# Turning the first half's results with transposing DMA transfers in a fused convolution and feed-forward kernel

## The chip, the cores and the metric

The kernel runs on one core of a Trainium2 chip. The metric is the time of one execution on the device in microseconds (us), as the median of a few runs; lower is better. One further execution was recorded by the profiler.

## What is computed

The input x is 32 sequences of 64 channels by 1024 positions. A state-space layer first convolves each channel along the sequence with a kernel that is generated from a few parameters, masked by each sequence's length. Its result, seen as 2048 tokens of 1024 values, goes through a gated feed-forward layer with 4-bit weights in groups of 128:

```python
gate = x2 @ Wg          # 1024 -> 2752
up = x2 @ Wu
inter = gate * jax.nn.sigmoid(gate) * up
out = (inter @ Wd).astype(jnp.float16)
x = x + out             # the residual: the layer's input, float32
```

`Wg`, `Wu` and `Wd` are unpacked as `q * s[group] - (z[group] + 1) * s[group]`. Only the last cast, to float16, and the residual sum matter for this change.

## The kernel before

**Stages.** Up to about 180 us the kernel generates the convolution kernels and convolves. From there to about 1160 us it runs the feed-forward layer, on two halves of 1024 tokens one after the other (`hf` 0 and 1). Each half has `NT` = 22 tiles of 128 intermediate columns (the last, `TAIL`, has 64), so there are `TILES` = 44 tiles `tau`. A tile has eight steps `g`. In each step TensorE issues four matmuls of `gate(tau, g)`, four of `down` for a unit that lies `LAG` = 11 steps back, and four of `up(tau, g)`. A number n = 8 tau + g - 11 counts the steps of `down`.

**Down units.** A unit is one block of 128 output columns (`hid`) for all 1024 tokens of the half. TensorE writes it into one of two PSUM buffers, `down_ps[0]` and `down_ps[1]`, in turn. VectorE takes it (`take_down`: multiply by the scale, add to `acc`) and signals `down_taken`. TensorE may begin a unit when the unit two before it is taken. `acc` has the output columns on the partitions and the tokens along the row.

**The first half's results.** After tile 21's units, GpSimd casts `acc` to float16 in `o16` (`cast_out`, 8 blocks), while VectorE starts the second half's sums in `acc`. `o16` still has output columns on the partitions; the output wants tokens there. So `turn_out(j)`, j = 0 to 3, has TensorE transpose two blocks of 128 tokens, 8 transposes of 128x128 each, into a `down_ps` buffer. Such a turn is put between a `down` unit and the `up` matmuls, at n = `TURN_AT` + 8 j (181, 189, 197, 205), which is step g = 0 of tiles 24 to 27. It counts as a unit of `down_ps`, hence `down_at` and `turn_at`. VectorE's `finish(j)` adds the two turned blocks to x, which lies in the four slots of `x_fin`, and SP stores them and loads the next two blocks of x.

**VectorE in a tile.** In each step it takes one down unit. After it, by step: g = 0 is preceded by `multiply` (sil times up); g = 1, 3, 5 unpack the next gate, up and down weights (`shift`); g = 2, 4, 6 subtract their zero points (`center`) and write the weights.

**SP's queue.** One queue issues every load and store of this stage, in the program's order. For each tile it loads gate weights for tile tau + 1, up weights, and down weights of tile tau: a transfer of 512 KB (`q_in`) and one of 256 KB (`z_in`) each, into a ring of `QRING` = 4 slots. A load waits until the load four before it has been centered (`centered`). After tile tau's loads, in tiles 25 to 28, come the stores of two finished blocks and loads of two further blocks of x (those of x up to block 7).

Of the kernel before, what the change touches and what calls it, by code (L numbers as in the profile page):

```python
# [9 lines left out]
F16 = mybir.dt.float16  # L10
# [3 lines left out]
ALU = mybir.AluOpType  # L14
ACT = mybir.ActivationFunctionType

P = 128
# [16 lines left out]
NT = 22  # L34
# [3 lines left out]
NH = HID // P  # L38
ROWS = G * NT
LAG = 11  # L40
QRING = 4
TURN_AT, TURN_STEP = 181, 8
SPLIT_FROM = 4
TINY = float(2.0 ** -60)

# [60 lines left out]
    return tau - tau // NT  # L106


def turns_before(n):

    return sum(TURN_AT + TURN_STEP * j < n for j in range(4))


def down_at(tau, hid):

    n = NH * tau + hid
    return n + turns_before(n)


def turn_at(j):  # L120
    return TURN_AT + TURN_STEP * j + 1 + j


def up_after(tau):
# [34 lines left out]
def build_program(nc, x, itok, log_dt, C, log_A, A_imag, D, gq, gs, gz, uq, us, uz, dq, ds, dz,  # L159
# [5 lines left out]
    with ExitStack() as ctx:  # L165
        def sb(name, shape, dt=F32):
            return ctx.enter_context(nc.sbuf_tensor(name, shape, dt))

        def sem(name):
            return ctx.enter_context(nc.semaphore(name))  # L170
# [75 lines left out]
        z_in += [sb(f"z_in{i}", [P, G, P], BF16) for i in range(2, QRING)]  # L246
        w["d"][1] = sb("wd1", [P, HID], F32R)
        staged = sb("staged", [P, HALF], F32R)

        ai_loaded, c_loaded, d_loaded = sem("ai_loaded"), sem("c_loaded"), sem("d_loaded")  # L250
        tab_in, ident_in_sb, lens_in = sem("tab_in"), sem("ident_in_sb"), sem("lens_in")
# [27 lines left out]
        down_mm, down_taken = sem("down_mm"), sem("down_taken")  # L279
        high_staged, high_stored, low_ready = sem("high_staged"), sem("high_stored"), sem("low_ready")  # L280
        high_in = [sem(f"high_in{i}") for i in range(KT)]
        o16_done = sem("o16_done")
        x_fin_in = [sem(f"x_fin_in{i}") for i in range(8)]
        last_mid, last_high, last_low = sem("last_mid"), sem("last_high"), sem("last_low")
        last_mm, last_taken = sem("last_mm"), sem("last_taken")
# [52 lines left out]
        def _(sp):  # L338
# [126 lines left out]
            def load_x(hf, tt):  # L465
                sp.dma_start(x_slot(hf, tt), x_rows(hf * HALF_G + tt)).then_inc(x_fin_in[tt if hf else tt % 4], 16)

            def store_out(hf, tt):
                dst = bass.AP(out.tensor, (hf * HALF_G + tt) * (HG * L), [[H * L, B], [L, HG], [1, L]])
                sp.dma_start(dst, x_slot(hf, tt)).then_inc(out_stored[tt % 4], 16)  # L470

            sp.wait_ge(x1_split, HALF_G)
            sp.wait_ge(scales_ready, 1)
            load_weights("d", 0)
# [2 lines left out]
            for tau in range(1, TILES):  # L477
                if tau + 1 < TILES:
                    load_weights("g", tau + 1)
                if up_after(tau) is not None:  # L480
                    load_weights("u", up_after(tau))
                if tau == NT:
                    sp.wait_ge(high_stored, 16 * KT)
                    for kt in range(KT):
                        sp.wait_ge(gate_mm, 2 * (G * TAIL + kt) + 2)
                        sp.dma_start(high[:, kt, :].bitcast(F32), high_back[kt]).then_inc(high_in[kt], 16)
                load_weights("d", tau)
                if SPLIT_FROM <= tau < SPLIT_FROM + KT:
                    sp.wait_ge(high_staged, tau - SPLIT_FROM + 1)
                    sp.dma_start(high_back[tau - SPLIT_FROM], staged[:].bitcast(F32)).then_inc(high_stored, 16)  # L490
                if tau == NT:
                    for tt in range(4):
                        load_x(0, tt)
                if NT + 3 <= tau < NT + 7:
                    for tt in range(2 * (tau - NT - 3), 2 * (tau - NT - 3) + 2):
                        if tt % 2 == 0:
                            sp.wait_ge(out_ready, tt // 2 + 1)
                        else:
                            sp.wait_ge(down_taken, turn_at(tt // 2) + 1)
                        store_out(0, tt)  # L500
                        if 2 <= tt < 6:
                            sp.wait_ge(out_stored[tt - 2], 16)
                            load_x(0, tt + 2)

            for tt in range(4):
                sp.wait_ge(out_stored[tt], 16 * 2)
# [220 lines left out]
        def _(dve):  # L727
# [281 lines left out]
                to = x_slot(1, tt)  # L1009
                dve.tensor_tensor(to, last_turn_ps(tt), to, ALU.add).then_inc(last_added, 1)  # L1010

            def finish(j):

                at = turn_at(j)
                dve.wait_ge(down_mm, at + 1)
                for i in range(2):
                    tt = 2 * j + i
                    dve.wait_ge(x_fin_in[tt % 4], 16 * (tt // 4 + 1))
                    to = x_slot(0, tt)
                    dve.tensor_tensor(to, down_ps[at % 2][:, i, :].bitcast(F16), to, ALU.add  # L1020
                                      ).then_inc(out_ready if i == 0 else down_taken, 1)

            dve.wait_ge(tab_in, 16)
            arguments(0)
# [33 lines left out]
            for tau in range(TILES):  # L1058
                for g in range(G):
                    if g == 0 and tau and tau != NT:  # L1060
                        multiply(tau - 1)
                    if g == G - 1 and tau == TAIL:
                        multiply(tau)
                    if g == G - 1 and tau == LAST:
                        multiply_last(0)
                        multiply_last(1)
                    n = G * tau + g - LAG
                    if n >= 0:
                        take_down(n // NH, n % NH)
                    if g == 5 and tau == TAIL:  # L1070
                        shift("d", TAIL)
                    if g == 0 and tau == NT:
                        center("d", TAIL)
                    if TURN_AT <= n < TURN_AT + 4 * TURN_STEP and (n - TURN_AT) % TURN_STEP == 0:
                        finish((n - TURN_AT) // TURN_STEP)
                    if tau == 0:
                        if g < G - 1:
                            scale_first_up(g)
                        if g < 6:
                            m, at = (("d", 0), ("g", 1), ("u", 1))[g // 2]  # L1080
                            if g % 2 == 0:
                                shift(m, at)
                            else:
                                center(m, at)
                        continue
                    if tau + 1 < TILES:
                        if g == 1:
                            shift("g", tau + 1)
                        if g == 2:
                            center("g", tau + 1)  # L1090
                    if up_after(tau) is not None:
                        if g == 3:
                            shift("u", up_after(tau))
                        if g == 4:
                            center("u", up_after(tau))
                    if tau == TILES - 1:
                        if g == 1:
                            shift("d", tau)
                        if g == 2:
                            center("d", tau)  # L1100
                    elif not is_tail(tau):
                        if g == 5:
                            shift("d", tau)
                        if g == 6:
                            center("d", tau)
# [9 lines left out]
        def _(pe):  # L1115
# [172 lines left out]
            def rows_second(tt):  # L1288

                taken_before(NH)  # L1290
                for hid in range(NH):
                    mm = pe.matmul(sum_ps(tt)[:, hid // 4, P * (hid % 4):P * (hid % 4) + P],
                                   o16[:, hid, P * tt:P * tt + P], ident16[:], start=False, stop=True,
                                   skip_group_check=True)
                mm.then_inc(sum_mm, 1)
# [5 lines left out]
                    mm = pe.transpose(last_turn_ps(tt)[:, P * hid:P * hid + P], o16[:, hid, P * tt:P * tt + P], ident16[:])  # L1301
                mm.then_inc(last_turned, 1)

            def turn_out(j):

                at = turn_at(j)
                if j == 0:
                    pe.wait_ge(o16_done, NH)
                    pe.wait_ge(ident16_ready, 1)
                pe.wait_ge(down_taken, at - 1)  # L1310
                for i in range(2):
                    to = down_ps[at % 2][:, i, :].bitcast(F16)
                    for hid in range(NH):
                        mm = pe.transpose(to[:, P * hid:P * hid + P],  # L1314
                                          o16[:, hid, P * (2 * j + i):P * (2 * j + i) + P], ident16[:])
                mm.then_inc(down_mm, 1)

            pe.wait_ge(k_sb_ready, NCH)
            for tau in range(TILES):
                for g in range(G):  # L1320
                    n = G * tau + g - LAG
                    if tau == NT and g == 0:
                        down(n // NH, n % NH)
                        gate(tau, g)
                    else:
                        gate(tau, g)
                        if n >= 0:
                            down(n // NH, n % NH)
                    if TURN_AT <= n < TURN_AT + 4 * TURN_STEP and (n - TURN_AT) % TURN_STEP == 0:
                        turn_out((n - TURN_AT) // TURN_STEP)  # L1330
                    if not is_tail(tau):
                        up(tau, g)
            for hid in range(NH - 3, NH):
# [50 lines left out]
```

## Time and profile before

| | |
|---|---|
| Median of 3 runs | 1186.89 us (1185.52 to 1187.82) |
| The profiled execution's own time | 1186.11 us |
| Its span in the trace | 1184.3 us |
| TensorE busy | 1155.2 us (98%) |
| VectorE busy | 891.4 us (75%) |
| ScalarE busy | 848.6 us (72%) |
| DMA queue of SP | 172.95 MB, 50.8% of 16 engines |

A matmul's duration overlaps with the next one's, so the time that TensorE spends on a piece of work is read from the starts of the instructions around it, not from the durations. "SPq" is SP's issuing of a transfer; the time "to landing" runs from the issue to the end of the transfer. The time of a transfer's issue is taken on SP, in which nothing else is issued.

### The profile page before, as it was taken

The numbers are of one execution on the slowest core, as the hardware profiler recorded it, in microseconds if no ns is written. First come the engines' busy times: TensorE is split into PE (matmuls) and PEld (weight loads), VectorE is DVE, ScalarE is ACT, GpSimd is POOL, SyncE is SP. The second block draws the span as 40 slices with busy tenths as digits, with TensorE's granted clock in tenths as the row PEclk, the third lists the DMA queues.
The fourth block names the chain that finished last, engine by engine and source line by source line (L and its number), as shares of the span: only waits on it lengthen the run. The fifth ranks groups of instructions, "written<-read, shape, count | busy, mean of one in ns | idle before, by whom it ended". The sixth has DMA issues, their size and how long they took to land.

```text
span 1184.3 us, 15015 instructions
## 1 busy us (share of the span) xinstructions
PE 1155.2 (98%) x5562; PEld 952.6 (80%) x5562; DVE 891.4 (75%) x964; ACT 848.6 (72%) x1396; POOL 221.0 (19%) x136
## 2 busy tenths in 40 slices
PE   5899999999999999999999999999999999999996
PEld 4899998788788878878878878888888888888883
DVE  6698854777777777777777898887777777777775
ACT  6533212888788788788878797778788788788773
POOL 0022000211332332121121241211211211211213
PEclk9899999999999999999999999999999999999999
DMA  8587868531464366434443775555434434444514
GB/s 296 159 267 247 286 200 266 145 81 54 116 162 114 108 163 158 130 100 107 107 107 95 239 206 153 163 177 143 107 103 111 107 103 111 107 101 113 151 48 166
DMA packets 66975, 173.94 MB, mean 147 GB/s; under 512 B 11654, under 2 KB 17222, under 8 KB 66902
## 3 DMA queue, kind: packets, MB, share of 16 engines
q1 hardware_dynamic: 66870, 172.95, 50.8%
q8 instruction: 44, 0.72, 0.2%
q14 instruction: 29, 0.24, 0.1%
q0 software_dynamic: 32, 0.03, 0.0%
HBM read 159.94 MB, written 15.83 MB: 148 GB/s over the span
## 4 chain that ended last, share of the span: by engine, by line
PE 92%; SPq 3%; DVE 2%; DMA 1%; issue 1%; POOL 0%; ACT 0%; DVEq 0%; POOLq 0%
PE pair L1211 27%; PE pair L1232 26%; PE pair L1252 26%; PE pair L1166 10%; DMA toep<-kernel_padded 1%; SPq L352 1%; DMA kernel_padded<-k_sb 0%; PE pair L1146 0%; POOL o L591 0%; DVE arg L746 0%; DVE y_nat L881 0%; PE pair L1281 0%; PE pair L1314 0%; SPq L377 0%; DVE turns L841 0%
## 5 line engine op out<-in xcount | busy, mean ns | idle before, releaser
L985 DVE SCALAR_TENSOR_TENSOR acc<-pair,s_down,acc 128x1024 f32<-128x1024 f32 x328 | 420.5, 1283 | 197.8 <-PE pair L1252 197.4
L667 ACT ACTIVATE pair<-pair,ratio 128x512 f32<-128x512 f32 x616 | 381.7, 665 | 100.5 <-PE pair L1211 100.2
L686 ACT ACTIVATE pair<-pair,ratio 128x512 f32<-128x512 f32 x581 | 360.2, 659 | 122.0 <-PE pair L1232 121.9
L1211 PE MATMUL pair<-high,wg 128*128 128x512 f32 x704 | 278.8, 396 | 0.0
L1211 PE MATMUL pair<-low,wg 128*128 128x512 f32 x704 | 276.5, 393 | 0.0
L1232 PE MATMUL pair<-high,wu 128*128 128x512 f32 x672 | 267.7, 398 | 0.4 <-DVE sil L963 0.4
L1252 PE MATMUL pair<-mid_h,wd 128*128 128x512 f32 x688 | 267.7, 391 | 0.0
L1252 PE MATMUL pair<-mid_l,wd 128*128 128x512 f32 x672 | 264.7, 394 | 0.0
L1232 PE MATMUL pair<-low,wu 128*128 128x512 f32 x672 | 263.2, 392 | 0.0
L543 POOL CAST mid_h<-sil 128x1024 fp32r<-128x1024 f32 (+1 forms) x43 | 45.1, 1049 | 695.7 <-DVE sil L963 685.0
L1211 PEld LDWEIGHTS pair<-high,wg 128*128 128x128 f32 x704 | 132.1, 188 | 31.7 <-ACT pair L667 1.1
L1232 PEld LDWEIGHTS pair<-high,wu 128*128 128x128 f32 x672 | 126.1, 188 | 38.5 <-issue 10.6
L1211 PEld LDWEIGHTS pair<-low,wg 128*128 128x128 f32 x704 | 132.8, 189 | 29.3
L1166 PE MATMUL pair<-u_all,toep 128*128 128x256 f32 (+7 forms) x1024 | 151.7, 310 | 4.5 <-DMA toep<-kernel_padded 4.5
L1166 PEld LDWEIGHTS pair<-u_all,toep 128*128 128x128 f32 x1024 | 147.0, 193 | 8.8 <-DMA toep<-kernel_padded 4.9
L1252 PEld LDWEIGHTS pair<-mid_h,wd 128*128 128x128 f32 x688 | 129.1, 188 | 30.1
L1252 PEld LDWEIGHTS pair<-mid_l,wd 128*128 128x128 f32 x672 | 126.2, 188 | 29.3
L1232 PEld LDWEIGHTS pair<-low,wu 128*128 128x128 f32 x672 | 126.3, 188 | 27.1
L923 DVE TENSOR_SCALAR q_in<-q_in,shifts 128x1024 int32<-128x1024 int32 x130 | 97.9, 753 | 6.4 <-DMA z_in<-zeros_plus_one 6.4
L546 POOL TENSOR_TENSOR mid_l<-sil,mid_h 128x1024 fp32r<-128x1024 f32 x42 | 101.9, 2425 | 3.4
L678 ACT ACTIVATE sil<-pair,ratio 128x512 f32<-128x512 f32 (+1 forms) x88 | 55.7, 692 | 1.4 <-PE pair L1211 1.3
L947 DVE TENSOR_TENSOR wg<-q_in,z_in 128x1024 fp32r<-128x1024 int32 x44 | 54.8, 1244 | 0.1
(157 smaller groups left out, 598.8 us busy)
## 6 DMA issues: line engine op xcount, KB each, us to landing
q_in<-rows_backwards SPq DMA_DIRECT2D x86, 512.0 KB, 4.6
z_in<-zeros_plus_one SPq DMA_DIRECT2D x130, 256.0 KB, 4.7
toep<-kernel_padded SPq DMA_DIRECT2D x64, 512.0 KB, 6.7
q_in<-_L_ffn_down_qweight_dram SPq DMA_DIRECT2D x42, 512.0 KB, 4.8
u_all<-in_x_dram SPq DMA_DIRECT2D x16, 512.0 KB, 10.0
x_fin<-in_x_dram SPq DMA_DIRECT2D x12, 512.0 KB, 8.3
out_dram<-x_fin SPq DMA_DIRECT2D x12, 512.0 KB, 5.3
high_parts<-staged SPq DMA_DIRECT2D x8, 512.0 KB, 3.0
```

The source lines that it names most:

```text
L543: pool.tensor_copy(mid_h[0:n, tau % 2], whole).then_inc(midh_done, 1)
L546: pool.tensor_tensor(low, whole, mid_h[0:n, tau % 2].bitcast(F32), ALU.subtract).then_inc(midl_done, 1)
L667: act.activation(gate_ps[:, tb, :], gate_ps[:, tb, :], ACT.Copy, scale=ratio[:, 0, G * t + g:G * t + g + 1]).then_inc(gate_scaled, 1)
L678: act.activation(sil[to:to + n, tb, :], gate_ps[0:n, tb, :], ACT.Silu, scale=ratio[0:n, 0, G * t + G - 1:G * t + G]).then_inc(gate_scaled, 1)
L686: act.activation(up_ps(tau)[:, tb, :], up_ps(tau)[:, tb, :], ACT.Copy, scale=ratio[:, 1, G * t + g:G * t + g + 1]).then_inc(up_scaled, 1)
L923: dve.tensor_scalar(q_in[slot][:], q_in[slot][:], shifts[:, m == "d":1 + (m == "d")], 15, ALU.logical_shift_right, ALU.bitwise_and).then_i ...
L947: dve.tensor_tensor(to, q, z, ALU.subtract).then_inc(centered, 1)
L985: dve.scalar_tensor_tensor(out=acc[:, hid, :], in0=ps, scalar=scale, in1=acc[:, hid, :], op0=ALU.mult, op1=ALU.add).then_inc(down_taken, 1)
L1166: mm = pe.matmul(conv_ps[half_][k][:, base + B * d:base + 256], toep[:, slot, P * (KT - 1 - d):P * (KT - d)], u_all[:, g, 0:KT - d, B * hh ...
L1211: mm = pe.matmul(gate_ps[:, tb, :], w["g"][tau % 2][:, g, :], rows[:, g, 512 * tb:512 * tb + 512], start=g == 0 and part == 0, stop=part = ...
L1232: mm = pe.matmul(up_ps(tau)[:, tb, :], w["u"][full_before(tau) % 2][:, g, :], rows[:, g, 512 * tb:512 * tb + 512], start=g == 0 and part = ...
L1252: mm = pe.matmul(unit_ps(tau, hid)[:, tb, :], w["d"][tau % 2][:, P * hid:P * hid + P], mid[:, tau % 2, 512 * tb:512 * tb + 512], start=par ...
```

## The change

The four turns leave TensorE. SP issues eight transposing DMA transfers for each of them instead, one for each block of output columns, from `o16` (SBUF) into a new SBUF buffer `turned` (two blocks of tokens, 4 KB a partition). One call turns [128 columns, 256 tokens] into two blocks of [128 tokens, 128 columns], 64 KB. The buffer is single: the next pair is turned after VectorE has finished the last one. `finish` is now called for one block at a time, in steps g = 1 and g = 3 of tiles 26 to 29, and reads `turned` in place of PSUM. The stores and x loads stand behind the waits for these.

```diff
-TURN_AT, TURN_STEP = 181, 8
 def down_at(tau, hid):
-    n = NH * tau + hid
-    return n + turns_before(n)
+    return NH * tau + hid
...
+        turned = sb("turned", [P, 2, HID], F16)
...
+            def turn_and_store(j):
+                if j == 0:
+                    sp.wait_ge(o16_done, NH)
+                else:
+                    sp.wait_ge(out_ready, 2 * j)
+                    for tt in (2 * j - 2, 2 * j - 1):
+                        store_out(0, tt)
+                if j < 4:
+                    for hid in range(NH):
+                        sp.dma_start_transpose(turned[:, :, P * hid:P * hid + P], o16[:, hid, 2 * P * j:2 * P * j + 2 * P]
+                                               ).then_inc(turned_in, 16)
+                if 2 <= j < 4:
+                    for tt in (2 * j, 2 * j + 1):
+                        sp.wait_ge(out_stored[tt % 4], 16)
+                        load_x(0, tt)
...
-                if NT + 3 <= tau < NT + 7:
-                    for tt in range(2 * (tau - NT - 3), 2 * (tau - NT - 3) + 2):
-                        if tt % 2 == 0:
-                            sp.wait_ge(out_ready, tt // 2 + 1)
-                        else:
-                            sp.wait_ge(down_taken, turn_at(tt // 2) + 1)
-                        store_out(0, tt)
-                        if 2 <= tt < 6:
-                            sp.wait_ge(out_stored[tt - 2], 16)
-                            load_x(0, tt + 2)
+                if NT + 3 <= tau <= NT + 7:
+                    turn_and_store(tau - NT - 3)
...
-            def finish(j):
-                at = turn_at(j)
-                dve.wait_ge(down_mm, at + 1)
-                for i in range(2):
-                    tt = 2 * j + i
-                    dve.wait_ge(x_fin_in[tt % 4], 16 * (tt // 4 + 1))
-                    to = x_slot(0, tt)
-                    dve.tensor_tensor(to, down_ps[at % 2][:, i, :].bitcast(F16), to, ALU.add
-                                      ).then_inc(out_ready if i == 0 else down_taken, 1)
+            def finish(tt):
+                dve.wait_ge(turned_in, 16 * NH * (tt // 2 + 1))
+                dve.wait_ge(x_fin_in[tt % 4], 16 * (tt // 4 + 1))
+                to = x_slot(0, tt)
+                dve.tensor_tensor(to, turned[:, tt % 2], to, ALU.add).then_inc(out_ready, 1)
...
-                    if TURN_AT <= n < TURN_AT + 4 * TURN_STEP and (n - TURN_AT) % TURN_STEP == 0:
-                        finish((n - TURN_AT) // TURN_STEP)
+                    if g in (1, 3) and NT + 4 <= tau < NT + 8:
+                        finish(2 * (tau - NT - 4) + g // 2)
...
-                    if TURN_AT <= n < TURN_AT + 4 * TURN_STEP and (n - TURN_AT) % TURN_STEP == 0:
-                        turn_out((n - TURN_AT) // TURN_STEP)
```

`turn_out` goes away whole; TensorE's wait for `ident16_ready`, which it held, moves to `rows_second(0)` at the end of the kernel, where the identity has long been there.

## Rows read from the trace of the kernel before

**Rows 1.** The page: span, busy times (first line), the chain that ended last.

```profile
span 1184.3 us, 15015 instructions
PE 1155.2 (98%) x5562; PEld 952.6 (80%) x5562; DVE 891.4 (75%) x964; ACT 848.6 (72%) x1396; POOL 221.0 (19%) x136
...
PE 92%; SPq 3%; DVE 2%; DMA 1%; issue 1%; POOL 0%; ACT 0%; DVEq 0%; POOLq 0%
```

**Rows 2.** Busy time by stretch: two tiles with a turn, two without.

```profile
714.31:737.35 23.04, 23.04 (x114) 18.84 (x113) 19.11 (x17) 18.07 (x31) 3.45 (x2) 1.00 0.45 129
737.35:760.40 23.05, 23.05 (x113) 18.75 (x112) 19.11 (x17) 17.97 (x31) 3.44 (x2) 1.00 0.51 141
...
806.50:828.80 22.30, 22.30 (x98) 17.95 (x97) 16.84 (x15) 18.01 (x31) 3.45 (x2) 1.00 0.48 130
828.80:851.10 22.30, 22.30 (x97) 17.95 (x96) 16.84 (x15) 18.01 (x31) 3.45 (x2) 1.00 0.42 107
```

**Rows 3.** TensorE's timeline at the second turn (start, duration, engine, line, operation).

```profile
739.81 0.39 PE L1252 MATMUL pair<-mid_l,wd 128*128 128x512 f32 x1
740.04 1.07 PE L1314 MATMUL pair<-ident,o 128*128 128x128 f16 x16
740.91 0.48 PE L1232 MATMUL pair<-high,wu 128*128 128x512 f32 x1
741.23 0.39 PE L1232 MATMUL pair<-low,wu 128*128 128x512 f32 x1
```

**Rows 4.** TensorE's timeline at the same step of tile 28.

```profile
808.34 0.39 PE L1252 MATMUL pair<-mid_h,wd 128*128 128x512 f32 x1
...
809.03 0.40 PE L1252 MATMUL pair<-mid_l,wd 128*128 128x512 f32 x1
809.31 0.47 PE L1232 MATMUL pair<-high,wu 128*128 128x512 f32 x1
809.62 0.39 PE L1232 MATMUL pair<-low,wu 128*128 128x512 f32 x1
```

**Rows 5.** Lines 1020 and 947 on VectorE: count, shortest/median/longest in ns.

```profile
L1020 DVE TENSOR_TENSOR x_fin<-pair,x_fin x8: 1214/1215/1225, 718.5 to 789.0; 128x1024 f32<-128x1024 f16 x8
...
L947 DVE TENSOR_TENSOR wg<-q_in,z_in x44: 1207/1215/1869, 180.6 to 1127.6; 128x1024 fp32r<-128x1024 int32 x44
```

**Rows 6.** VectorE's timeline in tile 28, from step g = 0.

```profile
809.46 1.28 DVE L985 SCALAR_TENSOR_TENSOR acc<-pair,s_down,acc 128x1024 f32<-128x1024 f32 x1 [0.30 <-PE pair L1252]
812.36 1.28 DVE L985 SCALAR_TENSOR_TENSOR acc<-pair,s_down,acc 128x1024 f32<-128x1024 f32 x1 [1.61 <-PE pair L1252]
813.56 0.74 DVE L923 TENSOR_SCALAR q_in<-q_in,shifts 128x1024 int32<-128x1024 int32 x1
815.13 1.28 DVE L985 SCALAR_TENSOR_TENSOR acc<-pair,s_down,acc 128x1024 f32<-128x1024 f32 x1 [0.83 <-PE pair L1252]
816.33 1.22 DVE L947 TENSOR_TENSOR wg<-q_in,z_in 128x1024 fp32r<-128x1024 int32 x1
817.90 1.28 DVE L985 SCALAR_TENSOR_TENSOR acc<-pair,s_down,acc 128x1024 f32<-128x1024 f32 x1 [0.36 <-PE pair L1252]
```

**Rows 7.** SP's issues in the profile's timeline, stores, x loads and a gate load.

```profile
732.92 1.29 SPq L470 DMA_DIRECT2D out_dram<-x_fin  x2
...
783.26 0.82 SPq L436 DMA_DIRECT2D q_in<-rows_backwards  x1
784.13 0.62 SPq L439 DMA_DIRECT2D z_in<-zeros_plus_one  x1
```

**Rows 8.** The page's DMA issues: count, KB each, median us to landing.

```profile
q_in<-rows_backwards SPq DMA_DIRECT2D x86, 512.0 KB, 4.6
z_in<-zeros_plus_one SPq DMA_DIRECT2D x130, 256.0 KB, 4.7
...
high_parts<-staged SPq DMA_DIRECT2D x8, 512.0 KB, 3.0
...
ident<-identity SPq DMA_DIRECT2D x1, 64.0 KB, 3.6
```

**Rows 9.** Issues of two shapes on SP: shortest/median/longest in ns.

```profile
L436 SPq DMA_DIRECT2D q_in<-rows_backwards x86: 520/527/822, 170.0 to 1095.3; - x86
L409 SPq DMA_DIRECT2D rows_backwards<-_L_ffn_gate_qweight_dram x16: 764/770/830, 58.3 to 128.0; - x16
```

**Rows 10.** Busy time by stretch: the densest DMA of this stage (last two columns: share, GB/s).

```profile
763.50:766.50 3.00, 3.00 (x25) 2.58 (x23) 2.30 (x2) 1.70 (x3) 2.92 (x2) 1.00 1.05 292
```

More of the change, by code:

```diff
@@ L106, in full_before @@
     return tau - tau // NT
-def turns_before(n):
-    return sum(TURN_AT + TURN_STEP * j < n for j in range(4))
 def down_at(tau, hid):
-    n = NH * tau + hid
-    return n + turns_before(n)
-def turn_at(j):
-    return TURN_AT + TURN_STEP * j + 1 + j
+    return NH * tau + hid
 def up_after(tau):
@@ L281, in build_program @@
         high_in = [sem(f"high_in{i}") for i in range(KT)]
-        o16_done = sem("o16_done")
+        o16_done, turned_in = sem("o16_done"), sem("turned_in")
         x_fin_in = [sem(f"x_fin_in{i}") for i in range(8)]
@@ L1290, in rows_second @@
                 taken_before(NH)
+                if tt == 0:
+                    pe.wait_ge(ident16_ready, 1)
                 for hid in range(NH):
@@ L1302, in turn_last @@
                 mm.then_inc(last_turned, 1)
[L1304 to L1316, printed above, removed]
             pe.wait_ge(k_sb_ready, NCH)
```

## The prediction

> **What bounds the kernel now.** I read the page's busy times and the chain that ended last first: TensorE is busy 98% of the span and holds 92% of the chain [rows 1]. So a saving counts only if it shortens TensorE's sequence, and an addition on another engine costs only if TensorE comes to wait for it. Next I cut the stage around the turns into stretches of one tile. The reader should see that TensorE is busy for the whole of each, at a granted clock of 1.00, and that a tile with a turn lasts 23.04 us and one without 22.30 us [rows 2]. Then come the timelines of TensorE, VectorE and SP in one tile, which tell what a turn displaces and what slack the others have.
>
> **What is removed from TensorE.** In place of a pitch of 0.23 us the 16 transposes take 740.04 to 740.91, and the first matmul behind them another 0.32 us until the next one starts [rows 3]. From the start of the last down matmul to the start of the second up matmul it is 741.23 - 739.81 = 1.42 us. Without a turn the same two are 809.62 - 809.03 = 0.59 us apart, which is 0.13 us more than two pitches [rows 4]: the first up matmul waits there for VectorE's product, and a turn covers this small wait. So locally a turn costs 0.83 us. Over the whole tile it is 23.04 - 22.30 = 0.74 us, since the matmuls of a tile without a turn run a little less densely [rows 2]. I take the whole tile: 4 x 0.74 = 2.96 us saved. The other end, if the 0.13 us and the rest did not come back, is 0.96 us a turn (1.42 less two pitches of 0.23), 3.84 us in all.
>
> **VectorE's finishes.** They stay eight additions of 1.22 us. Before they read PSUM; an addition of the same size with both operands in SBUF takes 1.22 us as well [rows 5]. So the total stays, and what changes is the place: g = 1 and g = 3, each beside an unpacking. I count from a, the start of the take in step g = 1 (812.36 in rows 6). Take to next operation is 1.20 us, the finish 1.22, the shift 0.74, so the take of g = 2 starts at a + 3.2 against 2.77 in the trace. With the center of 1.22 us behind it the take of g = 3 starts at a + 5.7 against 5.54; its finish ends at a + 8.1, the shift at a + 8.8, and the take of g = 4 is 0.5 us late, which the next steps give back [rows 6]. What lateness TensorE bears: a unit starts at 808.34 and its take ends at 809.46 + 1.28 = 810.74, 2.4 us later; the unit that needs its buffer starts two steps of 2.77 us later, at 5.5 us [rows 4, 6]. That leaves 3.1 us, and 2.6 us when 0.5 is used. Cost on TensorE: none. If that cover were gone, each of the eight finishes could cost up to 1.22 us, 9.8 us in all.
>
> **What the transposing transfers must fit into.** Turn 0 is issued behind tile 25's loads, which wait only for tile 24's centers, and finish(0) comes in tile 26: more than a tile of cover. The other three are tight, since `turned` is single. SP waits at `out_ready` until a + 8.1. Behind this wait in its queue stand two stores, eight transposing transfers, in turns 2 and 3 two loads of x, and then the gate weights for the next tile. Before, SP did not wait for VectorE's finishes in the tile itself, so those loads went out a good half tile earlier. VectorE needs the turned blocks at its next g = 1, at a + 22.3 + 1.2 = a + 23.5, and the gate weights one finish later, at a + 24.7. So there are 15.4 us for the first and 16.6 us for the second; call D the time that the eight transfers take in the queue.
>
> Turn 1: two stores are issued in 1.29 us [rows 7], then D, then the q and z transfers, 0.6 + 4.7 us to landing [rows 7, 8]: 6.6 + D. VectorE is late from D = 10.0, TensorE loses from D = 12.6. Turns 2 and 3: the other transfers are 4 of 512 KB plus 768 KB, 2.88 MB, at the densest rate of this stage, 292 GB/s [rows 10], 9.9 us. I add 1.2 us for the tail of the last one (a 512 KB transfer that lands in 3.0 us [rows 8] less its 1.8 us at that rate). So 11.1 + D: VectorE is late from D = 5.5, TensorE loses from D = 8.1. The x loads ahead of the gate weights meet their own deadline earlier. The stage moves about 0.5 MB more per turn, at 22.3 us a tile with the DMA engines at half their share [rows 2]; that alone costs nothing.
>
> **The size of D.** No transposing transfer is in this trace. Below: eight plain issues of 0.53 us [rows 9], 4.2 us, with 512 KB of data (1.8 us) beside them. Above: each as slow by itself as the one plain 64 KB load, 3.6 us [rows 8], one after the other, 28.8 us. Between them I take the row whose transfer is also cut into short pieces, issued in 0.77 us [rows 9]: D = 8 x 0.77 = 6.2 us. VectorE is then 0.7 us late in turns 2 and 3 and TensorE loses nothing. At the upper end turn 1 loses 6.6 + 28.8 - 16.6 - 2.6 = 16.2 us and turns 2 and 3 lose 20.7 us each, 57.6 us.
>
> Of the price, the row shows that TensorE turns a block of 128x128 in 0.87 / 16 = 0.054 us inside a stream [rows 3], and nothing of the DMA's way. The Trainium skill speaks against the change (VectorE: DVE Perf Modes, "The three transpose paths"): 390 ns for such a block on TensorE and 1309 ns by DMA. The trace has the first at a seventh of that, so these are times of a block alone and not rates. Were the 1309 ns a rate, a turn of 16 blocks would take an estimated 20.9 us, and by the same bounds 8.3 + 2 x 12.8 us would be lost and 2.96 saved, 1217.8 us. Another of its pages (DMA: Bandwidth & Descriptors, "Latency and other measured facts") has 261 GB/s for a transposing transfer, an estimated 2.0 us a turn, which would leave the issues as the bound and the sum at 2.96 us saved. No row here tells the two apart.
>
> **The sum.** The profiled execution took 1186.11 us, of it 1184.3 in the span. Less 2.96 us it is 1183.15 us. The median of the runs is 0.78 us above the profiled one, so I predict 1183.9 us, 0.25% below 1186.89.
>
> **The rivals.**
>
> *The transfers are slow, and the wait moves to SP's queue* (the other side). Place: the unpacking of the gate weights and the finish in step g = 1 of tiles 27 to 29. It decides from D = 9.6 us, 1.2 us a transfer: there turns 2 and 3 lose 1.5 us each, all of the saving. For it: eight operations in a row on one queue, ahead of the weights, each perhaps holding SP until its data have moved; and no row shows such an operation. Against it: the bytes are few, and plain issues are below 0.8 us. At half the upper bound, D = 14.4 us, turn 1 loses 1.8 and turns 2 and 3 lose 6.3 us each: 14.4 - 2.96 = 11.4 us more, 1198.3 us.
>
> *The transfers are somewhat slow, and the saving is given back.* At D = 10 us turns 2 and 3 lose 1.9 us each, and the time is 1186.89 - 2.96 + 3.8 = 1187.7 us, no change that can be measured.
>
> *The saving is smaller because the turns lay in a stall.* The turn covers a wait of 0.13 us that shows without it. If VectorE were still 0.3 us late at the product in each of tiles 26 to 29, the first up matmul would wait that much longer, and 1.2 us of the 2.96 would be gone: 1185.1 us. Against it: VectorE's lateness of 0.5 us falls by the idle time of each step, 0.83 us beside a shift and 0.36 us beside a center [rows 6], so it is gone before the product.
>
> **How the numbers follow.** No change is anything within 0.2%, 2.4 us, about what a measurement of this kernel can tell. My forecast, no loss on TensorE, has 0.60; somewhat slow, 0.13; slow, 0.19; a smaller saving, 0.08. Even in the forecast's case the saving of 2.96 us is only 0.6 us beyond the bound, and runs of one kernel differ by as much as 2.3 us, so I give a quarter of it to no change. Faster: 0.45 and a little of the smaller saving, 0.47. No change: 0.15 + 0.13 and most of the smaller saving, less a part of the somewhat slow case that ends above, 0.31. Slower: 0.22. The likeliest case's own range is 1182.5 to 1185.3. The range of 8 in 10 starts at 1182.3 and takes in the somewhat slow case and the nearer part of the slow one, up to 1194 (D near 13 us).
>
> **What the profile of the changed kernel would show.** Tiles 24 to 27 last 22.3 us instead of 23.04, and tiles 26 to 29 also. The eight transposing issues take 4 to 8 us on SP, and the gate weights behind them are there when VectorE reaches its g = 1 shift, or less than 2.6 us later. VectorE's eight finishes stay at 1.22 us. Wrong would be: tiles 27 to 29 longer than 22.3 us, VectorE waiting several us at the finish or at the shift for a DMA, and TensorE waiting for `take_down`; an addition from two SBUF operands that is far from 1.22 us; or all the transfers' issues above 1.2 us.

## The result and the profile after

The changed kernel takes 1196.3 us (median of 4, 1194.39 to 1198.82) against 1186.2 us before: a ratio of 1.0091, interval 1.0073 to 1.0109. It is slower by 0.9%, where 0.25% faster was forecast, and lies above the range (1182.3 to 1194 us). When the same kernel was run again, beside the kernel before, the ratio was 1.0065 (1.005 to 1.008). The profiled execution took 1198.82 us, 1197.0 of it in the span, and so is the longest of the four. The page of the changed kernel: busy times, the chain that ended last by engine, and the two groups in which new idle time stands.

```profile
span 1197.0 us, 14922 instructions
...
PE 1155.3 (97%) x5498; PEld 950.2 (79%) x5498; DVE 890.5 (74%) x964; ACT 848.6 (71%) x1396; POOL 221.1 (18%) x136
...
PE 85%; SPq 6%; DVE 3%; DMA 3%; issue 1%; ACT 0%; DVEq 0%
...
L1247 PE MATMUL pair<-mid_h,wd 128*128 128x512 f32 x688 | 269.2, 393 | 10.4 <-DVE acc L984 10.4
...
L922 DVE TENSOR_SCALAR q_in<-q_in,shifts 128x1024 int32<-128x1024 int32 x130 | 98.0, 754 | 18.6 <-DMA z_in<-zeros_plus_one 18.6
```

Against [rows 1], TensorE is busy as long as before with 64 transposes less, its share of the chain fell from 92% to 85%, and SP's queue and the DMA took over the difference. TensorE waited 10.4 us for takes, and VectorE's unpacking waited 18.6 us for weights, of it 11.8 us in this stage.

Busy time by stretch, one tile each (start and end, length, then busy time and count of TensorE, its weight loads, VectorE, ScalarE and GpSimd; the last three numbers are the granted clock, the DMA share and GB/s):

```profile
713.98:736.28 22.30, 22.30 (x97) 17.94 (x96) 16.84 (x15) 18.00 (x31) 3.45 (x2) 1.00 0.45 115
736.28:758.58 22.30, 22.30 (x97) 17.94 (x96) 16.84 (x15) 18.01 (x31) 3.45 (x2) 1.00 0.48 121
758.58:780.88 22.30, 22.30 (x97) 17.95 (x96) 18.94 (x17) 18.01 (x31) 3.46 (x2) 1.00 0.18 60
780.88:803.20 22.32, 22.32 (x97) 17.95 (x96) 18.43 (x17) 18.03 (x31) 3.45 (x2) 1.00 0.68 174
803.20:831.44 28.24, 23.81 (x97) 18.83 (x96) 19.06 (x18) 17.98 (x31) 3.45 (x2) 0.94 0.67 177
831.44:861.62 30.18, 24.24 (x97) 19.18 (x96) 18.97 (x18) 18.11 (x31) 3.45 (x2) 0.89 0.70 186
```

The four tiles that had a turn now last 22.30 to 22.32 us against 23.04 [rows 2]: the saving is there. Tiles 28 and 29 last 28.24 and 30.18 us instead of 22.30. SP's issues in the timeline show why, for turn 1 and turn 2:

```profile
772.46 1.29 SPq L460 DMA_DIRECT2D out_dram<-x_fin  x2
773.79 11.11 SPq L472 DMA_TRANSPOSE turned<-o  x8
784.95 0.59 SPq L426 DMA_DIRECT2D q_in<-rows_backwards  x1
785.58 0.58 SPq L429 DMA_DIRECT2D z_in<-zeros_plus_one  x1
...
796.38 1.86 SPq L460 DMA_DIRECT2D out_dram<-x_fin  x2
798.29 10.50 SPq L472 DMA_TRANSPOSE turned<-o  x8
808.83 1.24 SPq L456 DMA_DIRECT2D x_fin<-in_x_dram  x2
810.12 0.60 SPq L426 DMA_DIRECT2D q_in<-rows_backwards  x1
810.76 0.59 SPq L429 DMA_DIRECT2D z_in<-zeros_plus_one  x1
```

Eight transposing issues hold SP for 10.5 to 12.2 us, and nothing behind them is issued in that time. VectorE's timeline in tile 28 has what follows, and TensorE's has the end of it, here and in tile 29:

```profile
809.11 1.28 DVE L984 SCALAR_TENSOR_TENSOR acc<-pair,s_down,acc 128x1024 f32<-128x1024 f32 x1 [1.64 <-PE pair L1247]
813.11 1.23 DVE L1016 TENSOR_TENSOR x_fin<-turned,x_fin 128x1024 f32<-128x1024 f16 x1 [2.72 <-DMA x_fin<-in_x_dram]
818.89 0.75 DVE L922 TENSOR_SCALAR q_in<-q_in,shifts 128x1024 int32<-128x1024 int32 x1 [4.55 <-DMA z_in<-zeros_plus_one]
819.56 1.28 DVE L984 SCALAR_TENSOR_TENSOR acc<-pair,s_down,acc 128x1024 f32<-128x1024 f32 x1
```

```profile
816.07 0.40 PE L1206 MATMUL pair<-low,wg 128*128 128x512 f32 x1
820.89 0.80 PE L1247 MATMUL pair<-mid_h,wd 128*128 128x512 f32 x1 [4.43 <-DVE acc L984]
821.49 0.63 PE L1247 MATMUL pair<-mid_l,wd 128*128 128x512 f32 x1
...
844.29 0.40 PE L1206 MATMUL pair<-low,wg 128*128 128x512 f32 x1
850.62 0.79 PE L1247 MATMUL pair<-mid_h,wd 128*128 128x512 f32 x1 [5.94 <-DVE acc L984]
```

The pair to read is the finish at 813.11, late by x, and the shift at 818.89, late by the gate weights. The take at 819.56 is the one that TensorE's unit at 820.89 waits for. Its matmuls are then mostly 0.42 to 0.43 us apart, the first pair 0.60, in place of 0.23.

**The difference of 12.7 us between the two spans, by stretches.** I measure from one start of VectorE's product (`multiply`) to another, the same instruction in both traces. Up to that in tile 24: -0.3 us. To that in tile 28: 89.24 against 92.16 us, -2.9. To that in tile 30: 58.42 against 44.61 us, +13.8. The next 13 tiles: 289.68 against 288.80, +0.9. The end: +1.3. The last two are no effect of the change that I can name: a quiet tile lasts 22.16 or 22.31 us in both kernels, in varying numbers, and in another profiled execution of the changed kernel (c_changed, below) the same two stretches were 0.8 and 1.8 us shorter than here. The stage itself, 10.9 us of the 12.7, is close to the 10.1 us between the medians. Of the 13.8, TensorE's two gaps in front of the down units are 4.82 + 6.33 us less two pitches of 0.23, 10.7 us, and the 16 intervals between the matmuls behind them sum to another 3.3 us more than at the usual pitch; the rest is 0.2 us shorter.

### The profile page after: what moved, and what is told of

The parts are those of the page before. It is cut to its first block, busy times and chain, and to the rows that moved or that the text cites. A ratio compares the mean times of both kernels' runs of the same rounds, so it can differ in the third digit from the quotient of the medians.

```text
span 1197.0 us, 14922 instructions
## 1 busy us (share of the span) xinstructions
PE 1155.3 (97%) x5498; PEld 950.2 (79%) x5498; DVE 890.5 (74%) x964; ACT 848.6 (71%) x1396; POOL 221.1 (18%) x136
## 4 chain that ended last, share of the span: by engine, by line
PE 85%; SPq 6%; DVE 3%; DMA 3%; issue 1%; ACT 0%; DVEq 0%
PE pair L1206 25%; PE pair L1227 24%; PE pair L1247 24%; PE pair L1161 10%; SPq L472 3%; DMA z_in<-zeros_plus_one 2%; DMA toep<-kernel_padded 1%; SPq L342 1%; PE pair L1276 1%; DVE acc L984 1%; DMA kernel_padded<-k_sb 0%; SPq L460 0%; PE pair L1141 0%; DVE arg L745 0%; DVE y_nat L880 0%
## 5 line engine op out<-in xcount | busy, mean ns | idle before, releaser
L1247 PE MATMUL pair<-mid_h,wd 128*128 128x512 f32 x688 | 269.2, 393 | 10.4 <-DVE acc L984 10.4
L922 DVE TENSOR_SCALAR q_in<-q_in,shifts 128x1024 int32<-128x1024 int32 x130 | 98.0, 754 | 18.6 <-DMA z_in<-zeros_plus_one 18.6
```

The costliest lines, as they stand in the source:

```text
L922: dve.tensor_scalar(q_in[slot][:], q_in[slot][:], shifts[:, m == "d":1 + (m == "d")], 15, ALU.logical_shift_right, ALU.bitwise_and).then_i ...
L1247: mm = pe.matmul(unit_ps(tau, hid)[:, tb, :], w["d"][tau % 2][:, P * hid:P * hid + P], mid[:, tau % 2, 512 * tb:512 * tb + 512], start=par ...
```

## The experiments

"Q" below is the theory that the eight issues hold SP's queue and so delay what stands behind them. The column "six tiles" is the time from the product in tile 24 to that in tile 30 in the profiled execution; it takes in all of the stage and leaves out the differences elsewhere.

| kernel | ratio to before, interval | six tiles, us | a turn's transfers hold SP, us |
|---|---|---|---|
| before | 1 | 136.77 | none |
| changed | 1.0091 (1.0073 to 1.0109) | 147.66 | 10.5 to 12.2 |
| c_changed, the same again | 1.0065 (1.005 to 1.008) | 145.09 | 10.8 to 11.9 |
| e1_no_transfers | 0.9965 (0.9953 to 0.9978) | 133.07 | none |
| e2_plain_copies | 0.9965 (0.9952 to 0.9978) | 133.38 | 5.4 to 6.6 |
| e3_gate_first | 0.9986 (0.997 to 1.0002) | 135.23 | 11.1 to 12.2 |
| e4_x_first | 0.9997 (0.9979 to 1.0015) | 136.92 | 11.1 to 11.8 |
| e5_both | 0.9967 (0.9954 to 0.9979) | 133.54 | 10.9 to 11.1 |
| e5_again, the same again | 0.9977 (0.9962 to 0.9992) | 133.23 | 10.8 to 11.8 |
| e6_blocks_of_one | 1.034 (1.0319 to 1.0361) | 177.53 | 20.8 to 22.2 |
| e8_four_transfers | 0.9969 (0.9953 to 0.9984) | 135.17 | 5.3 to 6.7 |
| e7_one_transfer | 0.9967 (0.9953 to 0.998) | 133.39 | 3.7 to 5.0 |
| e9_one_both | 0.9966 (0.9951 to 0.9981) | 132.93 | 3.8 to 5.0 |

**Without the transfers.**

```diff
-                if j < 4:
-                    for hid in range(NH):
-                        sp.dma_start_transpose(turned[:, :, P * hid:P * hid + P], o16[:, hid, 2 * P * j:2 * P * j + 2 * P]
-                                               ).then_inc(turned_in, 16)
...
+            pool.memset(turned[:], 0.0).then_inc(turned_in, 1)
...
-                dve.wait_ge(turned_in, 16 * NH * (tt // 2 + 1))
+                dve.wait_ge(turned_in, 1)
```

> The changed kernel with the 32 transposing transfers left out; the finishes add a buffer of zeros, so the first half's result is not added to x. Theory Q (SP's queue: the eight issues hold SP for about 11 us, and the gate weights behind them come late): no weights are late, TensorE never waits for a take, and the whole saving of 2.9 us shows: 1183.3 us. Rival P (place: two finishes beside the unpacking make VectorE late): TensorE still waits in tiles 28 and 29 and the time stays above 1186 us. Rival B (the transfers slow the others by contention) expects 1183.3 us as Q does.

Measured 0.9965, six tiles in 133.07 us, no wait of TensorE for a take. The saving on TensorE is real, and the finishes in g = 1 and g = 3 cost nothing. Rival P falls. The four tiles from product to product take 88.77 us against 92.16, 3.4 us less, between the two ends of 2.96 and 3.84 us in the prediction (three of the four last 22.15 or 22.16 us, where the tiles without a turn in [rows 2] last 22.30):

```profile
717.28:806.05 88.77, 88.77 (x386) 71.73 (x385) 71.56 (x66) 72.17 (x120) 13.78 (x8) 1.00 0.44 122
```

**Plain copies in place of transposing ones.**

```diff
-                        sp.dma_start_transpose(turned[:, :, P * hid:P * hid + P], o16[:, hid, 2 * P * j:2 * P * j + 2 * P]
-                                               ).then_inc(turned_in, 16)
+                        sp.dma_start(turned[:, :, P * hid:P * hid + P], o16[:, hid, 2 * P * j:2 * P * j + 2 * P].rearrange("p (a b) -> p a b", a=2)
+                                     ).then_inc(turned_in, 16)
```

> The changed kernel with each of the 32 transposing transfers replaced by a plain copy of the same bytes between the same buffers, so the first half's result is added unturned. Theory Q: eight plain issues take 4.5 to 5 us instead of 11; VectorE's wait at the gate weights is below 1.5 us a tile, TensorE loses nothing: 1183.3 us, within 1 us. If any eight transfers in front of the weights were too much (the bytes, or their number), it would be above 1190 us.

SP's issues in its timeline for two of the turns:

```profile
774.06 6.09 SPq L472 DMA_DIRECT2D turned<-o  x8
...
796.19 6.57 SPq L472 DMA_DIRECT2D turned<-o  x8
```

The same number of transfers and bytes, but 6.1 and 6.6 us in place of 11 (expected 4.5 to 5): VectorE waited 2.5 us for weights in all, 1.7 us of it once, where less than 1.5 was expected, and TensorE for nothing; ratio 0.9965 (0.9952 to 0.9978). This is also the forecast's own case: with D near 6.2 us, the value that I had chosen, the forecast's ratio of 0.9975 lies within the measured interval.

**One load ahead of the turn.** The position in SP's order, in e3:

```diff
                 if tau + 1 < TILES:
                     load_weights("g", tau + 1)
+                if NT + 4 <= tau <= NT + 8:
+                    turn_and_store(tau - NT - 4)
                 if up_after(tau) is not None:
...
-                if NT + 3 <= tau <= NT + 7:
-                    turn_and_store(tau - NT - 3)
```

> Computes the same as the changed kernel. Only SP's order differs: each turn stands one load later, behind the gate weights of the next tile but one; the x loads still follow the eight transposing transfers. Theory Q: the transposing issues stay at 1.25 to 1.4 us each, the gate weights are there in time, x comes about 1 us late, which VectorE's slack of 2.6 us takes: TensorE never waits, 1183.5 us. Rival B (contention in the DMA engines, not the order): the weights are as late as before, within 2 us of 1196 us. Rival P: unchanged at 1196 us.

Measured 0.9986 (0.997 to 1.0002). The transfers hold SP as long as before, and the time falls by nearly 1% with the order: rival B, contention whatever the order, falls. Not all came back. VectorE waited 5.0 us for x, 3.6 of it once, where I had said 1 us, and TensorE waited 0.6 us for a take and 0.8 us for the product, where I had said none:

```profile
827.64 1.28 DVE L984 SCALAR_TENSOR_TENSOR acc<-pair,s_down,acc 128x1024 f32<-128x1024 f32 x1 [1.61 <-PE pair L1247]
832.49 1.23 DVE L1016 TENSOR_TENSOR x_fin<-turned,x_fin 128x1024 f32<-128x1024 f16 x1 [3.57 <-DMA x_fin<-in_x_dram]
```

One tile of the six lasted 24.15 us for it.

**x ahead of the wait.** In e4:

```diff
             def turn_and_store(j):
+                if 2 <= j < 4:
+                    for tt in (2 * j, 2 * j + 1):
+                        sp.wait_ge(out_stored[tt % 4], 16)
+                        load_x(0, tt)
...
-                if 2 <= j < 4:
-                    for tt in (2 * j, 2 * j + 1):
-                        sp.wait_ge(out_stored[tt % 4], 16)
-                        load_x(0, tt)
```

> Computes the same as the changed kernel. Only the loads of x for the next pair move ahead of SP's wait for the finishes, so that only two stores and eight transposing transfers stand before the gate weights. Theory Q: all three tight turns look like turn 1 of the changed kernel (gate weights 1.8 us late, VectorE's lateness partly carried on): waits of 1.5 to 3 us for the weights in each, TensorE loses 0 to 1 us in all, 1183.5 to 1185 us. If x was never the matter, it stays within 2 us of 1196 us.

Measured 0.9997 (0.9979 to 1.0015): the loss is nearly gone, the saving does not show. VectorE waited for the weights in all three tight turns, 8.2 us in all (1.8, 3.1 and 3.4); the last two are above what I had said. TensorE waited 0.9 us for takes, and 1.9 us at the first up matmul for VectorE's product; I had said 0 to 1 us in all. So of the two things behind the eight issues neither alone is the cause; each is enough to cost part of the saving.

**Both.** e5 has the order of e3 and the x loads of e4.

> Computes the same as the changed kernel. Each turn stands behind the gate weights of the next tile but one, and the x loads for the next pair stand ahead of SP's wait for the finishes. Theory Q (SP's queue, held by the transposing issues): nothing that VectorE needs soon stands behind the eight issues any more; they still take 11 us a turn, VectorE waits less than 0.5 us in any place, TensorE never waits for a take, and the six tiles 24 to 29 last 133.3 us, as in the kernel without transfers: a ratio of 0.9965 to the kernel before. If the transfers cost something apart from the order, the ratio stays at or above that of the kernel with only the gate weights first, 0.9986.

Measured 0.9967 (0.9954 to 0.9979), six tiles in 133.54 us, SP held for 10.9 to 11.1 us a turn, no wait for x, weights or takes. Eight transposing transfers of 1.25 us thus cost nothing that was measured where nothing urgent stands behind them. One of its seven executions took 1906.5 us, at a mean granted clock of 0.559; the others took 1181.05 to 1184.74, at 0.990 to 0.996, and the ratio is theirs. I repeated it:

> The kernel with gate weights and x loads first once more, to see whether its saving repeats (0.9967) and whether the single execution of 1906.5 us among its seven comes again. Theory Q expects the saving and says nothing of such an execution; expected is none.

Twelve executions, 1179.88 to 1186.33 us, ratio 0.9977 (0.9962 to 0.9992), and none like that one. What lowered the clock there stays open.

**The changed kernel again.**

> The changed kernel once more, beside the others on one chip. Theory Q: eight issues in 10.5 to 12.5 us, TensorE waits some 5 and 6 us for takes in tiles 28 and 29, ratio 1.007 to 1.011 to the kernel before.

Measured 1.0065, just below the expected 1.007. TensorE waited for takes in the same two places, 4.5 and 2.8 us, less than the 5 and 6 expected, and 0.8 us for the product; eight issues held SP for 10.8 to 11.9 us, and the weights and x behind them were late as before.

**How the hold goes with a transfer's size.** Three kernels, all of the changed kernel's order. In e6 each transfer is cut in two:

```diff
                     for hid in range(NH):
-                        sp.dma_start_transpose(turned[:, :, P * hid:P * hid + P], o16[:, hid, 2 * P * j:2 * P * j + 2 * P]
-                                               ).then_inc(turned_in, 16)
+                        for i in range(2):
+                            at = P * (2 * j + i)
+                            sp.dma_start_transpose(turned[:, i, P * hid:P * hid + P], o16[:, hid, at:at + P]
+                                                   ).then_inc(turned_in, 16)
...
-                dve.wait_ge(turned_in, 16 * NH * (tt // 2 + 1))
+                dve.wait_ge(turned_in, 32 * NH * (tt // 2 + 1))
```

> Computes the same as the changed kernel, in the changed kernel's order, with each transposing transfer of two blocks cut into two of one block (16 a turn, 32 KB each). If the hold on SP is a fixed time for a transfer, 16 x 1.25 = 20 us a turn stand before the weights, 9 us more than in the changed kernel, and the three tight turns lose 9 us each beyond it: about 1196 + 9 + 7 + 9 = 1221 us. If the hold goes by the blocks, each is 0.65 us and the time is the changed kernel's, 1196 us within 2.

In e7 and e8 GpSimd writes its casts by pairs of token blocks, so that a turn's source is one run in each partition, and one transfer (or four) takes it all. Here e7:

```diff
-        turned = sb("turned", [P, 2, HID], F16)
+        turned = sb("turned", [P, 2 * NH, P], F16)
...
+        by_pair = o16[:].rearrange("p h n -> p (h n)").rearrange("p (j h t) -> p j h t", j=4, h=NH)
...
-                    for hid in range(NH):
-                        sp.dma_start_transpose(turned[:, :, P * hid:P * hid + P], o16[:, hid, 2 * P * j:2 * P * j + 2 * P]
+                    for part in range(1):
+                        few = slice(NH // 1 * part, NH // 1 * (part + 1))
+                        sp.dma_start_transpose(turned[:, 2 * few.start:2 * few.stop, :], by_pair[:, j, few, :].rearrange("p h t -> p (h t)")
                                                ).then_inc(turned_in, 16)
...
-                pool.tensor_copy(o16[:, hid, :], acc[:, hid, :]).then_inc(o16_done, 1)
+                pool.tensor_copy(by_pair[:, :, hid, :], acc[:, hid, :].rearrange("p (j t) -> p j t", j=4)).then_inc(o16_done, 1)
...
-                dve.wait_ge(turned_in, 16 * NH * (tt // 2 + 1))
+                dve.wait_ge(turned_in, 16 * 1 * (tt // 2 + 1))
...
-                dve.tensor_tensor(to, turned[:, tt % 2], to, ALU.add).then_inc(out_ready, 1)
+                rows = to.rearrange("p (h n) -> p h n", n=P)
+                both = turned[:].rearrange("p (h i) n -> p h i n", i=2)
+                dve.tensor_tensor(rows, both[:, :, tt % 2, :], rows, ALU.add).then_inc(out_ready, 1)
```

> As the kernel with one transfer a turn, but with four of 128 KB. Fixed cost: 4 x 1.25 = 5 us a turn, at most 0.5 us of waiting for the gate weights, TensorE loses nothing, ratio 0.9965. Cost by the data: 10 us, ratio near 1.007.

> Computes the same as the changed kernel, in the changed kernel's order of issues. GpSimd lays the cast results out by pairs of token blocks, so that one transposing transfer of 512 KB does a turn in place of eight of 64 KB. If each transfer costs SP a fixed time (1.25 us for one block as for two), a turn holds SP for 1.3 to 3 us, D falls below 5.5 us, VectorE waits for nothing and the whole saving shows: ratio 0.9965 to the kernel before, 1183 us. If the time goes by the data above two blocks, the turn still takes 10 us and the ratio stays near 1.007.

The lines of the transposing issue of e6, of the changed kernel, of e8 and of e7 (count, shortest/median/longest in ns), and e7's time from issue to landing:

```profile
L474 SPq DMA_TRANSPOSE turned<-o x64: 1211/1234/2200, 730.2 to 865.1; - x64
```

```profile
L472 SPq DMA_TRANSPOSE turned<-o x32: 1229/1247/2384, 731.8 to 835.5; - x32
```

```profile
L475 SPq DMA_TRANSPOSE turned<-o x16: 1262/1269/2792, 730.5 to 823.5; - x16
```

```profile
L475 SPq DMA_TRANSPOSE turned<-o x4: 3738/4166/5042, 730.9 to 817.0; - x4
...
DMA to landing us min/median/max: 5.6/5.9/6.9
```

The medians are 1.23 us for 32 KB, 1.25 for 64 KB, 1.27 for 128 KB and 4.17 us for 512 KB. Up to 128 KB the time is one for each transfer and does not depend on the data; it is neither the bytes nor the number of blocks. (In e7 and e8 the source's layout changed together with the size; e6 has the changed kernel's layout.) e6 confirms the mechanism in the other direction: 21 us a turn, ratio 1.034, 1226.9 us where 1221 was expected. e7 gives 0.9967 in the changed kernel's own order, with no wait of VectorE for a transfer in the stage. e8 gives 0.9969, though in its profile the third turn still held SP for 6.7 us and VectorE waited 4.9 us for weights in two places (at most 0.5 was expected); TensorE then lost 0.9 us at the product, and the six tiles took 135.17 us, some 2 us more than in e5, e7 and e9.

**Both remedies together.**

> One transfer a turn, with SP's order of the kernel that has the gate weights and the x loads first. Theory Q: with the order mended the number of transfers no longer matters, so the same ratio as that kernel, 0.9967 within 0.0012; nothing further is to be had, since TensorE waits for no take in either.

Measured 0.9966 (0.9951 to 0.9981). The intervals of e5, e7 and e9 overlap; there is one saving, and each remedy brings it back whole. No measured difference separates these three from one another, or from e8.

## Why the prediction was wrong, point by point

**What bounds the kernel; what is removed.** Right. 2.96 us were forecast, the four tiles gave 2.9 us in the changed kernel and 3.4 us in e1.

**VectorE's finishes.** Right: 1.22 us from SBUF as from PSUM (1215 to 1226 ns), and no cost from their place in e1.

**What the transfers must fit into.** The places were right: the gate weights and x behind the eight issues, in the step g = 1 of the tile after. The measure of it was right in part by luck, as told below. Turn 1 was 1.76 us late by the profile, against 6.6 + 11.1 - 16.6 = 1.1 by the formula. For turns 2 and 3, with the measured D of 10.5 and 12.2 us, the formula gives a landing 21.6 and 23.3 us behind `out_ready`; it was 818.89 - 796.38 = 22.5 and 848.62 - 824.33 = 24.3 us.

**The size of D: the step that failed.** I took 8 x 0.77 = 6.2 us, from a plain transfer in short pieces, as the nearest row; it was 10.5 to 12.2 us. The decision stood at 9.6 us, so with the right D the formula says slower. The row I chose was of another operation, and the plain copies of e2, at 5.4 to 6.6 us a turn, show that it is good for just that. With bounds of 4.2 and 28.8 us and a decision in between, 0.19 for the slow case was too little.

That number I had weighed and set aside: the Trainium skill (VectorE: DVE Perf Modes, "The three transpose paths") has 1309 ns for a block of 128x128 by DMA. I said that it was the time of a block alone and no rate, and this much is so: two and four blocks hold the queue for 1.25 and 1.27 us too. Read as a fixed time for each transfer on the queue, it would have given an estimated 10.5 us for eight, close to what was measured. Whether the Trainium skill's figure and the hold measured here are the same quantity is not shown: from issue to landing such a transfer took 2.4 us.

**What a late weight costs TensorE.** Even with D right my sum would have been too small: 11.1 + 10.5 - 19.2 = 2.4 and 11.1 + 12.2 - 19.2 = 4.1 us, 6.5 in all, against 13.8. Three terms were missing. First, the turns are not independent. In turn 2 the wait at `out_ready` ended at 796.38, 9.6 us behind the take of step g = 1 (786.77) and not 8.1, since VectorE was still late from turn 1, and in turn 3 the lost time was carried in the same way: 1.2 to 1.5 us less room in each. Second, the landing was 1 us later in each than my formula gives, and that it came so close is luck. I had counted the two stores' 1.05 MB beside D, 3.6 us at my rate of 292 GB/s; but they had landed by 801.1, while the eight issues held SP. Behind D the stretch up to the shift was longer than my rate gives for what I had counted there: 10.06 us in turn 2, in which 2.4 MB moved and not the 1.8 MB of x and the gate weights, since the loads of the next up and down weights, issued from 811.40, ran beside them.

```profile
808.83:818.89 10.06, 7.63 (x34) 5.85 (x32) 2.51 (x2) 7.54 (x13) 0.68 (x1) 1.00 0.88 241
```

With the shorter room and the measured landing VectorE is late by 7.4 and 8.9 us; its two waits are 2.72 + 4.55 = 7.27 and 3.33 + 5.45 = 8.78 us, and TensorE's idle time is 4.6 and 6.1, so that the slack of 2.6 us was right (2.7). Third, the clock. TensorE's granted clock around the end of each idle time, in stretches of 3 us:

```profile
818.00:821.00 3.00, 0.11 (x1) 0.11 (x1) 2.11 (x3) 0.00 (x0) 0.00 (x0) 0.89 1.05 228
821.00:824.00 3.00, 3.00 (x8) 2.37 (x9) 3.00 (x3) 0.14 (x1) 0.00 (x0) 0.54 0.83 187
824.00:827.00 3.00, 3.00 (x15) 2.46 (x14) 3.00 (x4) 2.62 (x5) 0.00 (x0) 1.00 0.52 201
...
849.00:852.00 3.00, 1.38 (x3) 1.16 (x4) 3.00 (x4) 0.00 (x0) 0.00 (x0) 0.50 0.99 229
852.00:855.00 3.00, 3.00 (x9) 2.34 (x8) 3.00 (x4) 1.22 (x2) 0.00 (x0) 0.59 0.08 27
```

It fell to the lower level, 0.50 (1.2 of 2.4 GHz), during the 4.6 and 6.1 us of idle time, and the 7 and 9 intervals between matmuls that follow sum to 3.3 us more than at 0.23 us each. The three terms add 2.7, 1.9 and 3.3 us to the 6.5, 14.4 in all against 13.8.

The clock's share is no fixed part of the idle time. In c_changed a wait of 4.5 us was followed by 14 intervals at the lower level, which cost 2.9 us, and one of 2.8 us by none, for the clock stayed at 1.00; in e6 waits of 8.9 and 14.1 us cost about 1.8 and 1.4 us behind them. The stretches behind the two waits of c_changed:

```profile
819.00:822.00 3.00, 2.98 (x7) 2.43 (x8) 3.00 (x3) 0.01 (x1) 0.00 (x0) 0.50 0.66 155
822.00:825.00 3.00, 3.00 (x8) 2.35 (x8) 3.00 (x4) 2.43 (x4) 0.00 (x0) 0.50 0.44 176
...
847.20:850.20 3.00, 3.00 (x13) 2.49 (x14) 3.00 (x3) 1.34 (x3) 0.00 (x0) 1.00 0.83 195
```

**The rivals.** The slow transfers happened: its place and its mechanism were as written, and its time at D = 14.4 us, 1198.3 us, was reached at D of 10.5 to 12.2 us because of the three missing terms, so that the two times lie 2 us apart by luck. The middle case, the saving given back at D = 10 us, did not happen. The rival of VectorE's lateness at the product did not happen in e1, but in e4 and e8, behind waits of 3.4 and 3.0 us for the weights, TensorE waited up to 0.9 us at the product. So the slack of 2.6 us at the takes is not the only one to ask for.

## What to carry to other kernels

Before work is handed to a queue that also feeds the bounding engine, ask what stands behind it and when that is needed; the same hold of 11 us cost 1% in one place of the order and nothing one load later (with x loaded ahead). For an operation that the trace does not show, a fixed time for each instruction belongs among the prices, beside the bytes; here it was the right one up to 128 KB, and one large transfer was cheaper than eight small ones. Issuing the transfers from a queue other than SP's was not tried. When a decision lies between two bounds, let the chance follow the distance to it, not the row that is easiest to defend.

## What was not expected of the hardware

A transposing transfer between SBUF buffers held the issuing queue for 1.23 to 1.27 us (medians) whether it turned one, two or four blocks of 128x128, twice the 0.62 us of a plain copy of the same bytes in e2 and more than twice the 0.53 us of a plain load [rows 9]. While eight of them run, the DMA engines are mostly idle; with one transfer for the whole turn they are full, at 221 GB/s. Both stretches below begin as the last store in front of the turn lands (777.15 and 776.28 us), and end before the data of the next loads move. The changed kernel first, then e7 (last columns: DMA share, GB/s):

```profile
777.00:780.00 3.00, 3.00 (x15) 2.44 (x14) 2.17 (x3) 2.62 (x6) 0.00 (x0) 1.00 0.29 59
780.00:783.00 3.00, 3.00 (x15) 2.44 (x14) 2.64 (x3) 1.73 (x4) 0.00 (x0) 1.00 0.24 51
```

```profile
776.00:778.00 2.00, 2.00 (x10) 1.64 (x9) 1.20 (x2) 1.65 (x4) 0.00 (x0) 1.00 1.15 221
```

The hold of SP for the single transfer was 3.7 to 5.0 us for 512 KB. At which size between 128 and 512 KB the time begins to go by the data was not tried.
